# A four-layer graph network: keys first, shorter masks, joint finishing, output by two tiles, and products with the counts ahead of those with the mask

## The chip, the cores and the metric

The kernel runs on one NeuronCore of a Trainium2 chip. The metric is the time of one execution on the device, in microseconds (us); lower is better. Besides TensorE (matrix products; its weight loads are shown apart, as PEld) the core has VectorE (DVE), ScalarE (ACT), GpSimd (POOL) and SyncE (SP), which here issues most transfers.

## What is computed

A graph of 2500 nodes (256 features each) and 40000 edges passes through four blocks, each `x = x + layer(relu(layernorm(x)))`: two graph-attention layers with 8 heads of 32 features, a product with a 256 x 256 matrix built from the edges, three neighbour-mean layers with three dense layers, and a graph attention with 4 heads of 64. The core of an attention, per head:

```python
e = leaky_relu(el[src] + er[dst], 0.2)
ex = exp(e - segment_max(e, dst)[dst])
out = segment_sum((ex / segment_sum(ex, dst)[dst])[:, None] * h[src], dst)
x = elu(out + b)
```

The last attention has `exp(-leaky_relu(s))` with the roles of `src` and `dst` exchanged, and its result passes through `elu` twice (once per head, once over all heads) before the residual is added.

## The kernel before, in words

Nodes are padded to 20 tiles of 128 (`NT`, 2560 = `NP`). The kernel keeps a dense matrix of edge counts, `C[s, d]`, in f16 in on-chip memory: 20 source tiles by 2560 destinations.

*Start and building of C.* A first stage (lines 166 to 397) loads the edges, turns them and makes a table. The next (lines 439 to 612) goes through 40 windows of 64 destinations; for each, VectorE makes one-hot tiles (`ohc`, `ohl`), three in a ring, and TensorE multiplies them into `acc`; ScalarE copies the window to C. The same stage finds repeated edges: SyncE loads the keys of one round, `right` and `left` (L508, L510), TensorE compares them in `psD` (L604, L606) ahead of the window's own products (`three`, L589), and GpSimd scatters weights. `rows_in` (L159) loads x on the same SyncE queue.

*Attention* (`attention`, L630), called three times. After a layer norm (or the ELU of the layer before) and the product with the weights, factors are prepared: for an edge the weight is a product of a source factor (U or V) and a destination factor (F1 or F2), and which pair applies depends on the sign of `el + er`. So the sum over sources is a product with a *mask*: counts where the sum is positive, zero elsewhere, and one with the *counts* for the rest. The loop (from L997) goes over heads h, over `PARTS` of the destinations (2 halves of 1280 in attention 1 and 2, 4 quarters of 640 in attention 3, where `split` is set), and over the 20 source tiles s:

- ScalarE compares: `Rm` = relu(rows + bias), a huge number where the sum is positive (L1067);
- VectorE makes the mask `M` = min(Rm, C) (L1111). In attention 1 and 2 every fourth tile is made by VectorE alone, in one longer operation (L1114), except those in `MORE_ON_ACT`. In attention 3 twelve of twenty tiles also get `Mn` = C - M (L1101); the other eight, `TURNED`, use a product with C itself;
- TensorE multiplies the mask (L1198) and, for attention 1 and 2, the counts (L1206; in attention 3 for the tiles in `TURNED`, L1201) into eight banks, four for each of two parts in turn, with high and low halves of the factors side by side.

`Rm` and `M` have `SG` buffers (4; 5 in attention 3). ScalarE may start tile s when the mask of tile s - SG is made, VectorE when TensorE has finished with tile s - SG. TensorE waits in `cut` for the mask of its tile, and its semaphore `s_P` tells that the tile is done.

When a part is through, its sums are evacuated inside the next part, after `LEAD` tiles: ScalarE scales the low halves into `tl` (L1075), VectorE adds the high halves (L1138), multiplies by F2 and F1 (L1142, L1143), adds (L1147), and divides by the sum of the weights (L1152, L1156, L1160), one step after each mask. In attention 1 and 2 the result of the first half waits in `stash` and is copied after the second (L1165), since it overwrites factors that are still read. ScalarE issues its instructions in the order LEAD comparisons, evacuation, the others.

*End.* `elu` (L1217) applies the last activation in batches of four tiles, in two rounds with an exponential each; `write_result` loads x back in one transfer of 2.5 MB and writes the output in six, on GpSimd's queue.

Of the kernel before, what the change touches and what calls it, by code (L numbers as in the profile page):

```python
# [15 lines left out]
P = 128  # L16
N = 2500
E = 40000
D = 256
# [18 lines left out]
MORE_ON_ACT = {(0, 7), (1, 11)}  # L38
# [29 lines left out]
def build(nc, x, src, dst, ew, gat0, gat1, sage, dec, gat3, out):  # L68
# [4 lines left out]
    with top:  # L73
# [365 lines left out]
        with Phase() as ph:  # L439
# [52 lines left out]
            def _(sp):  # L492
                rows_in(sp, XB, x, s_x)
                for l, (Wx, gat) in enumerate(((Wx0, gat0), (Wx1, gat1))):
                    sp.dma_start(Wx[:, :, 0:D], gat[0].rearrange("(k p) f -> p k f", p=P)).then_inc(s_w, 16)
                    for j in range(2):
                        sp.dma_start(av[:, l, j, :], gat[1 + j].rearrange("(a h) d -> a (h d)", a=1)
                                     .to_broadcast([P, D])).then_inc(s_w, 16)
                sp.dma_start(bias[:, :], gat0[3].rearrange("(a f) -> a f", a=1).to_broadcast([P, D])).then_inc(s_w, 16)
# [130 lines left out]
        def attention(Wx, first, nh, dh, split, norm, sgn, scatter, next_bias=None):  # L630
# [181 lines left out]
            with heads as hp:  # L812
# [4 lines left out]
                F1, F2 = hp.sb("F1", [P, TH], f32), hp.sb("F2", [P, TH], f32)  # L817
# [5 lines left out]
                with Phase() as ph:  # L823
# [61 lines left out]
                    def _(v):  # L885
# [38 lines left out]
                        ch.wait()  # L924
                        v.tensor_scalar(kap[:, :], kap[:, :], TOP * LO, None, ALU.mult).then_inc(s_e, 1)
# [23 lines left out]
                    def _(a):  # L949
# [7 lines left out]
                        a.activation(F1[:, :], tt[:, :], ACT.Exp).then_inc(s_ex, 1)  # L957
                        a.activation(F2[:, :], tt2[:, :], ACT.Exp).then_inc(s_ex, 1)
# [38 lines left out]
                with Phase() as ph:  # L997
# [3 lines left out]
                    tl = ph.sb("tl", [P, RG, cw if split else 2 * cw], f32)  # L1001
                    stash = None if split else ph.sb("stash", [P, TP, dh], f32)
                    q1 = ph.sb("q1", [P, TP, cw], f32)
                    rec = ph.sb("rec", [P, TP], f32)
                    if scatter:
# [3 lines left out]
                    s_R, s_M, s_Mn, s_cut, s_P, s_E, s_tl, s_v, s_bias = (  # L1009
                        ph.sem(n) for n in ("R", "M", "Mn", "cut", "P", "E", "tl", "v", "bias"))  # L1010
# [51 lines left out]
                    def _(a):  # L1062
                        def steps(h, p, s0, s1):
                            for s in range(s0, s1):
                                if s in on_act[p]:
                                    cut(a, h * PARTS + p, s - SG, hold)
                                    a.activation(Rm[:, s % SG, :], rows[:, p % 2, :], ACT.Relu,  # L1067
                                                 bias=cB[:, ds(h + s * nh, 1)]).then_inc(s_R, 1)

                        def evacuate(h, p):  # L1070
                            q = h * PARTS + p
                            hold(a, s_P, (q + 1) * NT + SG)
                            hold(a, s_E, q + 2)
                            for r, n, part in banks(p % 2, 1):
                                ins = a.activation(tl[:, r:r + n, :], part, ACT.Copy, scale=1 / LO)  # L1075
# [13 lines left out]
                    def _(v):  # L1089
# [3 lines left out]
                        v.sem_inc(s_E, 2)  # L1093
                        ch = Chain(v, s_v)

                        def low_part(h, p, s):
# [3 lines left out]
                            Cs = C[:, s * NP + p * W:s * NP + (p + 1) * W]  # L1100
                            v.tensor_tensor(Mn[:, u, :], Cs, M[:, u, :], ALU.subtract).then_inc(s_Mn, 1)  # L1101

                        def steps(h, p, s0, s1, between=()):
                            between = list(between)
                            for s in range(s0, s1):
                                g, u = (h * PARTS + p) * NT + s, s % SG
                                Cs = C[:, s * NP + p * W:s * NP + (p + 1) * W]
                                if s in on_act[p]:
                                    v.wait_ge(s_R, compared(h, p, s) + 1)
                                    v.wait_ge(s_P, g + 1)  # L1110
                                    v.tensor_tensor(M[:, u, :], Rm[:, u, :], Cs, ALU.min).then_inc(s_M if s in ONE else s_cut, 1)  # L1111
                                else:
                                    v.wait_ge(s_P, g + 1)
                                    v.scalar_tensor_tensor(M[:, u, :], rows[:, p % 2, :], cN[:, ds(h + s * nh, 1)], Cs,  # L1114
# [9 lines left out]
                        def evacuation(h, p):  # L1124

                            q = h * PARTS + p
                            factor = lambda Fq: Fq[:, :].rearrange("p (t h) -> p t h", h=nh)[
# [52 lines left out]
                        for stage in stages + last:  # L1180
                            stage()
# [1077 lines left out]
```

## Time and profile before

| | |
|---|---|
| median of 3 runs | 2196.62 us (2195.84 to 2196.69) |
| the profiled execution | 2193.83 us, its span 2192.2 us, mean granted clock 0.940 |
| busy | TensorE 1747.3 (80%), VectorE 1618.4 (74%), ScalarE 1410.0 (64%), GpSimd 299.0 (14%) |
| stages | start to the first window 46.0; C 295.7; attention 1 prepared 79.9, loop 345.0; attention 2 prepared 76.4, loop 344.5; matrix, neighbour and dense layers with preparation of attention 3 690.5; loop of attention 3 271.8; end 42.4 |

A row of a timeline gives the start of an instruction, its duration, engine, line, what it writes and reads, and how long the engine stood idle before it. Durations of neighbours overlap by their latency; the distance from start to start is what an instruction takes of its engine. A row with xN is N such instructions in a row. The share of busy time is a mean over all stages; what counts is which engine fills a stage.

### The profile page before, as it was taken

The page shows a single profiled execution, that of the slowest core. Times are in us where ns is not written, and L with a number is a line of the kernel's source. Part 1 is how long each engine was busy: PE and PEld are TensorE (multiplying, and loading weights), DVE is VectorE, ACT ScalarE, POOL GpSimd, SP SyncE. Part 2 cuts the span into 40 slices and gives each one's busy share as a digit, 9 for nine tenths or more (in the row PEclk, how much of TensorE's full clock was granted, in tenths as well). Part 3 has the DMA queues.
Part 4 walks back from the last instruction along what each step waited for, and adds up shares of the span by engine and source line. Part 5 has one row for each costly group of instructions (what it writes and reads, how often), then busy time and mean ns, then how long its engine had stood idle before and what let it go on. Part 6 is the DMA issues. An engine that isn't in the chain of part 4 may idle for free. (4 is left out here: it accounts for less than half of the span.)

```text
span 2192.2 us, 64066 instructions
## 1 busy us (share of the span) xinstructions
PE 1747.3 (80%) x21987; PEld 1343.4 (61%) x21987; DVE 1618.4 (74%) x3673; ACT 1410.0 (64%) x2346; POOL 299.0 (14%) x457
## 2 busy tenths in 40 slices
PE   2998886298998855989885499998989984688881
PEld 1333334288888735888884356665548973688881
DVE  4988877899999978999999722222332257899997
ACT  0146675799999849999996712221213355899992
POOL 2465500466400011000000000000000001000000
PEclk9999998699999987999998799999999997899996
DMA  3000000010110000101011110000001010000102
GB/s 85 1 1 2 2 2 1 27 39 26 38 38 27 14 26 16 38 27 39 26 38 35 67 42 1 0 0 7 1 21 33 22 56 13 14 20 21 27 15 95
DMA packets 32298, 54.99 MB, mean 25 GB/s; under 512 B 10541, under 2 KB 23626, under 8 KB 31800
## 3 DMA queue, kind: packets, MB, share of 16 engines
q1 hardware_dynamic: 27848, 46.45, 6.5%
q0 software_dynamic: 4208, 5.24, 0.7%
q8 instruction: 160, 2.62, 0.5%
q14 instruction: 82, 0.67, 0.1%
HBM read 43.19 MB, written 8.49 MB: 24 GB/s over the span
## 5 line engine op out<-in xcount | busy, mean ns | idle before, releaser
L1198 PE MATMUL ps<-R,M 128*128 128x132 f16 (+1 forms) x8640 | 808.8, 221 | 202.7 <-DVE M L1111 101.9
L1067 ACT ACTIVATE Rm<-rows,cB 128x1280 bf16<-128x1280 f32 (+1 forms) x832 | 884.3, 1153 | 20.3 <-DVE Mn L1101 13.8
L1198 PEld LDWEIGHTS ps<-R,M 128*128 128x128 f16 x8640 | 728.8, 97 | 245.6 <-issue 115.2
L1206 PE MATMUL ps<-HB,C 128*128 128x66 f16 x6400 | 596.1, 193 | 0.0
L1111 DVE TENSOR_TENSOR M<-Rm,C 128x1280 f16<-128x1280 bf16 (+1 forms) x832 | 555.3, 691 | 41.0 <-ACT Rm L1067 37.4
L1206 PEld LDWEIGHTS ps<-HB,C 128*128 128x128 f16 x6400 | 571.7, 97 | 0.0
L1630 PE MATMUL psA<-R,C 128*128 128x512 f16 (+1 forms) x1200 | 253.0, 350 | 20.3 <-POOL ones L1664 9.5
L558 DVE TENSOR_SCALAR ohc<-cells,near 128x1280 f16<-128x1280 f16 x387 | 213.2, 551 | 58.4 <-PE acc L596 54.8
L596 PE MATMUL acc<-ohc,ohl 128*128 128x420 f16 (+1 forms) x1161 | 244.2, 348 | 1.6 <-DVE ohl L560 0.4
L1114 DVE SCALAR_TENSOR_TENSOR M<-rows,cN,C 128x1280 f16<-128x1280 f32 x128 | 197.9, 1546 | 0.0
L1630 PEld LDWEIGHTS psA<-R,C 128*128 (+1 forms) x1200 | 118.7, 99 | 117.5 <-issue 33.2
L596 PEld LDWEIGHTS acc<-ohc,ohl 128*128 128x128 f16 x1161 | 89.9, 98 | 148.6 <-DVE ohl L560 94.1
L423 POOL DMA_INDIRECT wd<-wv,wi x104 | 123.2, 1185 | 128.3 <-issue 71.6
L542 ACT ACTIVATE C<-acc 128x420 f16<-128x420 f32 (+1 forms) x120 | 55.7, 542 | 125.0 <-PE acc L596 125.0
L1781 DVE TENSOR_SCALAR rdeg<-psD 128x1 f32 (+1 forms) x20 | 3.2, 158 | 153.0 <-ACT tl L1746 153.0
L560 DVE TENSOR_SCALAR ohl<-lows,bT 128x128 f16<-128x128 f16 x387 | 101.5, 262 | 0.0
L1560 ACT ACTIVATE R<-L 128x256 f32 (+3 forms) x40 | 14.5, 363 | 129.8 <-DVE L L1792 80.3
L1101 DVE TENSOR_TENSOR Mn<-C,M 128x640 f16<-128x640 f16 x192 | 93.5, 487 | 0.6
L1201 PE MATMUL ps<-VS,C 128*128 128x130 f16 x640 | 88.7, 222 | 0.0
L1198 PE MATMUL ps<-R,Mn 128*128 128x130 f16 x960 | 86.8, 220 | 0.0
L1754 ACT ACTIVATE hT<-ps,b0c 128x128 f32<-128x128 f32 x80 | 22.9, 368 | 86.9 <-PE ps L1705 86.9
L1705 PE MATMUL ps<-xT,W 128*128 128x128 f32 x640 | 76.3, 278 | 1.6 <-ACT xT L1750 1.6
(300 smaller groups left out, 2333.9 us busy)
## 6 DMA issues: line engine op xcount, KB each, us to landing
rows<-rowd SPq DMA_DIRECT2D x32, 640.0 KB, 3.9
rows<-rowd SPq DMA_DIRECT2D x16, 320.0 KB, 3.5
xd<-R SPq DMA_DIRECT2D x4, 640.0 KB, 2.9
xr<-xd SPq DMA_DIRECT2D x20, 128.0 KB, 2.0
xd<-HB SPq DMA_DIRECT2D x1, 2560.0 KB
xr<-xd POOLq DMA_DIRECT2D x1, 2560.0 KB, 9.2
R<-in_x SPq DMA_DIRECT2D x1, 2432.0 KB
xr<-in_x SPq DMA_DIRECT2D x19, 128.0 KB, 2.0
```

Of the source, the lines that this page charges most:

```text
L423: g.indirect_dma_start(out=wd[:, :], out_offset=bass.IndirectOffsetOnAxis(ap=m["wi"][w][:, :], axis=0), in_=m["wv"][w][:, :], in_offset=No ...
L558: v.tensor_scalar(ohc[:, u, :], cells[:, :], near[:, q % 2, ds(k, 1)], None, ALU.is_equal).then_inc(s_oh, 1)
L560: v.tensor_scalar(ohl[:, u, :], lows[:, :], bT[:, ds(k, 1)], None, ALU.is_equal).then_inc(s_oh, 1)
L596: ins = pe.matmul(bank(b, q % 2), ohl[:, u, :], ohc[:, u, d0 * NT:d1 * NT], start=first_, stop=True, skip_group_check=True)
L1067: a.activation(Rm[:, s % SG, :], rows[:, p % 2, :], ACT.Relu, bias=cB[:, ds(h + s * nh, 1)]).then_inc(s_R, 1)
L1101: v.tensor_tensor(Mn[:, u, :], Cs, M[:, u, :], ALU.subtract).then_inc(s_Mn, 1)
L1111: v.tensor_tensor(M[:, u, :], Rm[:, u, :], Cs, ALU.min).then_inc(s_M if s in ONE else s_cut, 1)
L1114: v.scalar_tensor_tensor(M[:, u, :], rows[:, p % 2, :], cN[:, ds(h + s * nh, 1)], Cs, ALU.is_gt, ALU.mult).then_inc(s_M, 1)
L1198: m = pe.matmul(region(p % 2, r), lhsT, rhs, start=first, stop=True, skip_group_check=True)
L1201: m = pe.matmul(region(p % 2, r), C[:, s * NP + p * W + (r % TP) * P:][:, 0:P], VS[:, TURNED.index(s), :, ds(h * cw, cw)], start=False, st ...
L1206: m = pe.matmul(both[:, :, cw:2 * cw], C[:, s * NP + p * W + r * P:][:, 0:P], VP[:, s, :, ds(h * cw, cw)], start=False, stop=True, skip_gr ...
L1630: m = pe.matmul(psA[:, :], lhsT, SPv[:, s, :, :].rearrange("p l c -> p (l c)"), start=s == 0, stop=s == NT - 1)
```

## The change

Five parts:

1. *Keys first*: SyncE issues the keys of the first two windows before x and the weights (`later_loads`).
2. *Shorter masks*: in the last part of each head, comparison and masks cover only the destinations that exist, `wide(p)`: 1220 in place of 1280, 580 in place of 640. The factors of the padding are made zero by two more small operations before the exponentials. TensorE still multiplies whole tiles; `MORE_ON_ACT` loses tile 11 of the second half, so VectorE makes that mask alone.
3. *Joint finishing*: `tl` holds two parts; the additions are still made for each part, the other steps once for two (the factors are one tensor, F12). `stash` and the copy from it are gone.
4. *Output by two tiles*: the last stage is a pipeline over ten pairs of tiles, with three activations on ScalarE and two operations on VectorE for each; x comes back in five transfers and the output leaves in eleven, all on SyncE's queue.
5. *Counts ahead of the mask*: TensorE makes a source tile's products with the counts first, and waits for the mask only then. In attention 3 the regions are also numbered by tile and side in turn.

```diff
-MORE_ON_ACT = {(0, 7), (1, 11)}
+MORE_ON_ACT = {(0, 7)}
...
-                rows_in(sp, XB, x, s_x)
-                for l, (Wx, gat) in enumerate(((Wx0, gat0), (Wx1, gat1))):
...
+                def later_loads():
+                    rows_in(sp, XB, x, s_x)
+                    for l, (Wx, gat) in enumerate(((Wx0, gat0), (Wx1, gat1))):
...
+                    if q == 1:
+                        later_loads()
...
+                        for q in (tt, tt2):
+                            ch(v.tensor_scalar(q[:, TH - nh:TH], q[:, TH - nh:TH], padneg[:, 0:1], None, ALU.add))
+                        ch.wait()
...
+                    wide = lambda p: W - (NP - N if p == PARTS - 1 else 0)
...
-                                    a.activation(Rm[:, s % SG, :], rows[:, p % 2, :], ACT.Relu,
+                                    a.activation(Rm[:, s % SG, 0:wide(p)], rows[:, p % 2, 0:wide(p)], ACT.Relu,
...
-                            hold(a, s_E, q + 2)
+                            hold(a, s_fin, h * (PARTS // 2) + p // 2 + 1)
...
-                                ch(v.tensor_tensor(xv, xv, factor(F2), ALU.mult))
-                                ch(v.tensor_tensor(q1[:, :, :], xu, factor(F1), ALU.mult))
+                                ch(v.tensor_tensor(both(tl), both(tl), factors, ALU.mult))
...
+                                ch(v.tensor_tensor(both(tl)[:, :, 0], both(tl)[:, :, 0], both(tl)[:, :, 1], ALU.add))
...
-                                ch(v.tensor_copy(room[:, 0:TP, ds(h * cw, dh)], stash[:, :, :]))
...
+                            return [add] + ([scale, total, weight, inverse, mean] if p % 2 else [])
...
+                                    for r in range(RG):
+                                        side, d = sides(r)
+                                        if split and side and s in TURNED:
+                                            pe.matmul(region(p % 2, r), Cd(d), VS[:, TURNED.index(s), :, ds(h * cw, cw)],
+                                                      start=False, stop=True, skip_group_check=True)
+                                        if not split:
+                                            both = region(p % 2, r).rearrange("p (l c) -> p l c", l=2)
+                                            pe.matmul(both[:, :, cw:2 * cw], Cd(d), VP[:, s, :, ds(h * cw, cw)],
+                                                      start=opens and r % 3 == 0, stop=True, skip_group_check=True)
                                     cut(pe, q, s, lambda eng, sem, value: eng.wait_ge(sem, value))
                                     for r in range(RG):
...
+                def negative(k):
+                    if k >= 4:
+                        a.wait_ge(s_u, k - 3)
+                    a.activation(e(k), of_heads(k), ACT.Relu, scale=-1.0).then_inc(s_r, 1)
+
+                def power(k):
+                    a.wait_ge(s_r, k + 1)
+                    a.activation(e(k), e(k), ACT.Exp, scale=-1.0).then_inc(s_e, 1)
+
+                def again(k):
+                    a.wait_ge(s_e, k + 1)
+                    a.activation(e(k), e(k), ACT.Exp, bias=minus[:, 0:1]).then_inc(s_ee, 1)
...
+                def unit(k):
+                    v.wait_ge(s_ee, k + 1)
+                    v.scalar_tensor_tensor(y(k).rearrange("p (h c) -> p h c", c=64), e(k), -1.0, of_heads(k), ALU.add,
+                                           ALU.max).then_inc(s_u, 1)
+
+                def residual(k):
+                    v.wait_ge(s_u, k + 1)
+                    if 2 * k % TB == 0:
+                        v.wait_ge(s_xr[2 * k // TB], 16)
+                    v.tensor_tensor(y(k), y(k), xr[:, 2 * k * D:(2 * k + 2) * D], ALU.add).then_inc(s_y, 1)
```

How the instructions stand. First SyncE at the beginning of the stage that builds C, before (`right` and `left` are the keys, `flat` their source, `R` takes x):

```order
L491 UNCONDITIONAL_BRANCH
L161 DMA R<-in_x 128x19x256
L163 DMA R<-in_x 68x256
L495 DMA Wx<-in_L_gnn_W 128x2x256
L497 DMA HB<-in_L_gnn_al 128x256
...
L499 DMA bias<-in_L_gnn_b 128x256
L462 TENSOR_LOAD table
...
L508 DMA right<-flat 2x512
L510 DMA left<-flat 4x128
```

and with the change:

```order
L491 UNCONDITIONAL_BRANCH
L462 TENSOR_LOAD table
...
L510 DMA right<-flat 2x512
L512 DMA left<-flat 4x128
...
L506 COMPARE_AND_BRANCH
L161 DMA R<-in_x 128x19x256
L163 DMA R<-in_x 68x256
L496 DMA Wx<-in_L_gnn_W 128x2x256
```

Two windows' keys now stand in front of the nine other loads. Next TensorE at the first source tile of attention 1, before (`HB` holds the factors that go with the counts `C`, `R` those that go with the mask `M`; ps00 to ps03 are the banks):

```order
L1198 MATMUL ps00_145<-R,M_131 128x132
L1206 MATMUL ps00_145<-HB,C 128x2x33
...
L1198 MATMUL ps01_146<-R,M_131 128x132
L1206 MATMUL ps01_146<-HB,C 128x2x33
...
L1198 MATMUL ps03_148<-R,M_131 128x132
L1206 MATMUL ps03_148<-HB,C 128x2x33
```

and with the change:

```order
L1205 MATMUL ps00_142<-HB,C 128x2x33 x3
L1205 MATMUL ps01_143<-HB,C 128x2x33 x3
L1205 MATMUL ps02_144<-HB,C 128x2x33 x3
L1205 MATMUL ps03_145<-HB,C 128x2x33
L1212 MATMUL ps00_142<-R,M_130 128x132 x3
L1212 MATMUL ps01_143<-R,M_130 128x132 x3
L1212 MATMUL ps02_144<-R,M_130 128x132 x3
L1212 MATMUL ps03_145<-R,M_130 128x132
```

Ten products with the counts, then ten with the mask, where one followed the other in turn. Last VectorE in the body of attention 1's loop over heads, in the first half, after five masks; before:

```order
L1138 TENSOR_TENSOR tl<-ps_152,tl 128x66
...
L1142 TENSOR_TENSOR tl<-tl,F_96 128x10x33
...
L1143 TENSOR_TENSOR q_134<-tl,F_95 128x330
...
L1147 TENSOR_TENSOR q_134<-q_134,tl 128x330
...
L1160 TENSOR_TENSOR R<-q_134,rec 128x10x32
...
L1165 COPY R<-stash 128x10x32
```

and with the change:

```order
L1146 TENSOR_TENSOR tl<-ps_149,tl 128x66
...
L1154 TENSOR_TENSOR tl<-tl,F_95 128x1320
...
L1158 TENSOR_TENSOR tl<-tl 128x20x33
...
L1170 TENSOR_TENSOR R<-tl,rec 128x20x32
```

Between the rows shown stand the masks of the running half, one after each step. The steps are fewer and twice to four times as long, and after the second half's additions (the other place) only masks follow.

## Rows read from the trace of the kernel before

**Rows 1.** Busy time by stage: stretch, length, busy us of each engine, granted clock, DMA.
```profile
421.60:766.60 345.00, 305.37 (x6400) 289.10 (x6400) 334.07 (x488) 335.80 (x320) 102.44 (x120) 0.98 0.09 29
...
1878.00:2149.80 271.80, 234.99 (x3840) 224.24 (x3840) 253.71 (x672) 248.04 (x384) 0.00 (x0) 0.98 0.07 20
2149.80:2192.20 42.40, 0.00 (x0) 0.00 (x0) 30.74 (x61) 10.46 (x10) 5.21 (x7) 0.50 0.31 122
```

**Rows 2.** Timeline of SyncE at the start: start, duration, what is issued.
```profile
30.85 0.40 SPq L161 DMA_DIRECT2D R<-in_x  x1
...
37.62 0.43 SPq L499 DMA_DIRECT2D bias<-in_L_gnn_b  x1
39.71 0.32 SPq L508 DMA_DIRECT2D right<-flat  x1
```

**Rows 3.** Timeline of TensorE at the start, idle time before it behind.
```profile
45.98 0.59 PE L604 MATMUL psD<-notlater,big 128*128 128x512 f16 x1 [26.32 <-DMA left<-flat]
```

**Rows 4.** DMA issues of the page: count, KB each, us from issue to landing.
```profile
xr<-xd SPq DMA_DIRECT2D x20, 128.0 KB, 2.0
...
xr<-xd POOLq DMA_DIRECT2D x1, 2560.0 KB, 9.2
```

**Rows 5.** Timeline of ScalarE, attention 1.
```profile
445.44 0.88 ACT L1075 ACTIVATE tl<-ps 128x198 f32<-128x198 f32 x4
...
467.48 20.16 ACT L1067 ACTIVATE Rm<-rows,cB 128x1280 bf16<-128x1280 f32 x16
487.66 0.91 ACT L1075 ACTIVATE tl<-ps 128x198 f32<-128x198 f32 x4
```

**Rows 6.** Timeline of VectorE, attention 1.
```profile
603.91 1.54 DVE L1114 SCALAR_TENSOR_TENSOR M<-rows,cN,C 128x1280 f16<-128x1280 f32 x1
605.37 2.29 DVE L1111 TENSOR_TENSOR M<-Rm,C 128x1280 f16<-128x1280 bf16 x3
...
617.15 1.03 DVE L1138 TENSOR_TENSOR tl<-ps,tl 128x198 f32<-128x198 f32 x4
618.10 0.81 DVE L1111 TENSOR_TENSOR M<-Rm,C 128x1280 f16<-128x1280 bf16 x1
618.83 0.49 DVE L1142 TENSOR_TENSOR tl<-tl,F 128x330 f32<-128x330 f32 x1
```

**Rows 7.** Timeline of TensorE, attention 1.
```profile
599.84 0.22 PE L1198 MATMUL ps<-R,M 128*128 128x132 f16 x1
599.89 0.19 PE L1206 MATMUL ps<-HB,C 128*128 128x66 f16 x1
599.92 0.22 PE L1198 MATMUL ps<-R,M 128*128 128x132 f16 x1
```

**Rows 8.** Timeline of TensorE's weight loads, attention 1.
```profile
599.89 0.10 PEld L1198 LDWEIGHTS ps<-R,M 128*128 128x128 f16 x1
```

**Rows 9.** Timeline of ScalarE, attention 3.
```profile
1946.03 0.85 ACT L1075 ACTIVATE tl<-ps 128x195 f32<-128x195 f32 x4
1946.78 5.14 ACT L1067 ACTIVATE Rm<-rows,cB 128x640 bf16<-128x640 f32 x7
1952.58 9.86 ACT L1067 ACTIVATE Rm<-rows,cB 128x640 bf16<-128x640 f32 x13 [0.66 <-DVE Mn L1101]
```

**Rows 10.** Timeline of VectorE, attention 3.
```profile
1945.30 0.89 DVE L1111 TENSOR_TENSOR M<-Rm,C 128x640 f16<-128x640 bf16 x2
```

**Rows 11.** Timeline of ScalarE, before attention 2.
```profile
770.34 0.42 ACT L744 ACTIVATE e<-z 128x256 f32<-128x256 f32 x1 [0.22 <-DVE z L684]
770.66 0.40 ACT L748 ACTIVATE e<-e 128x256 f32<-128x256 f32 x1
```

**Rows 12.** Timeline of ScalarE, last stage.
```profile
2152.36 2.00 ACT L1308 ACTIVATE e<-e 128x1024 f32<-128x1024 f32 x2 [6.25 <-DVE e L1262]
```

**Rows 13.** Timeline of VectorE, last stage.
```profile
2151.43 1.74 DVE L1262 TENSOR_SCALAR e<-HB 128x256 f32<-128x256 f32 x8 [1.60 <-PEq L101]
...
2184.86 1.23 DVE L1291 SCALAR_TENSOR_TENSOR R<-e,R 128x1024 f32<-128x1024 f32 x1
```

More of the change, by code:

```diff
@@ L1130, in evacuation @@
                             room = HB[:, 0:NT * nh * cw] if split else R[:, :]
                             room = room.rearrange("p (t c) -> p t c", t=NT)
-                            held = not split and p == 0
-                            o = stash[:, :, :] if held else room[:, p * TP:(p + 1) * TP, ds(h * cw, dh)]
                             def add():
                                 hold(v, s_tl, q + 1)
-                                for r, n, part in banks(p % 2, 0):
-                                    ch(v.tensor_tensor(tl[:, r:r + n, :], part, tl[:, r:r + n, :], ALU.add))
+                                parts = list(banks(p % 2, 0))
@@ L1149, in weight @@
                             def weight():
-                                hold(v, s_E, q + 3)
-                                ch(v.tensor_scalar(rec[:, :], q1[:, :, dh], 1e-30, None, ALU.max))
+                                ch.wait()
+                                ch(v.tensor_scalar(rec[:, :], both(tl)[:, :, 0, dh], 1e-30, None, ALU.max))
                             def inverse():
@@ L1159, in mean @@
                                 ch.wait()
-                                ch(v.tensor_tensor(o, q1[:, :, 0:dh], rec[:, :].unsqueeze(2).to_broadcast([P, TP, dh]),
-                                                   ALU.mult))
-                            def unstash():
-                                ch.wait()
-                                ch(v.tensor_copy(room[:, 0:TP, ds(h * cw, dh)], stash[:, :, :]))
-                            stages = [add, scale, both, weight, inverse, mean]
-                            return stages, [unstash] if not split and p == 1 else []
+                                v.tensor_tensor(room[:, some, ds(h * cw, dh)], both(tl)[:, :, 0, 0:dh],
+                                                rec[:, :].unsqueeze(2).to_broadcast([P, 2 * TP, dh]), ALU.mult).then_inc(s_fin, 1)
+                            return [add] + ([scale, total, weight, inverse, mean] if p % 2 else [])
                         def rest(h, p, before):
-                            stages, last = evacuation(*before) if before else ([], [])
-                            steps(h, p, LEAD, NT, stages + last)
+                            steps(h, p, LEAD, NT, evacuation(*before) if before else [])
                         body = parts_in_order(v, steps, rest)
                         with v.Fori(1, nh) as h:
-                            ch.begin(h - 1, PARTS * (NB + 5) + (0 if split else 1))
+                            ch.begin(h - 1, PARTS * (NB - 1) + PARTS // 2 * 4)
                             body(h, False)
                             ch.end(nh - 1)
-                        stages, last = evacuation(nh - 1, PARTS - 1)
-                        for stage in stages + last:
+                        for stage in evacuation(nh - 1, PARTS - 1):
                             stage()
@@ L1192, in _ @@
                                     cut(pe, q, s, lambda eng, sem, value: eng.wait_ge(sem, value))
                                     for r in range(RG):
-                                        first = s == 0 and r % 3 == 0
-                                        side = r // TP if split else 0
-                                        lhsT = (Mn if side and s in TWO else M)[:, s % SG, (r % TP) * P:(r % TP + 1) * P]
+                                        side, d = sides(r)
+                                        lhsT = (Mn if side and s in TWO else M)[:, s % SG, d * P:(d + 1) * P]
```

204 lines of the change are left out of this document (75 added, 129 removed).

## The prediction

> **What bounds the kernel now.** I read four views, in this order: the busy time of each engine by stage, the timelines of each engine inside a stage, the order of the instructions, and the waits. The stages first [rows 1]. In the first attention loop ScalarE is busy 335.80 of 345.00 us and VectorE 334.07, TensorE 305.37 at granted clock 0.98: two engines tie for the bound and TensorE has a tenth to spare. The second attention runs the same loop. In the third (1878.0 to 2149.8) VectorE and ScalarE are again ahead of TensorE, 253.71 and 248.04 of 271.8 us, and neither fills them. In the last stage (42.4 us) TensorE does nothing and VectorE works 30.74 us. The chain of waits of the page covers only that last stage, so it says nothing about the loops.
>
> At the start, SyncE issues the loads of x and of weights from 30.85 and comes to the first keys only at 39.71 [rows 2]; TensorE starts at 45.98, after 26.32 us of idleness that ended with the keys' landing [rows 3]. Nothing else is late there.
>
> **Keys first.** SyncE was free at 30.85 [rows 2]. It still has to read its table (the last earlier issue, 37.62, ended at 38.05 and the keys came at 39.71: 1.7 us), then issues three small transfers at about 0.35 us each, and they need to land. For the landing the bounds are 0 and the 5 us that it took behind 2.4 MB of x; the nearest row is a 128 KB piece with 2.0 us [rows 4], and I take 2.0. So 30.85 + 1.7 + 1.0 + 2.0 = 35.5 in place of 45.98: **-10.5 us**. The x load and weights now go behind the second keys; nobody needs them before the stage ends, and the next keys are asked for only after the first window's matrix products. They cost nothing; without that cover the cost would be the same 10 us again. What is late next is TensorE and VectorE themselves, which share this stage.
>
> **The loops of attention 1 and 2.** One head is two halves of ten destination tiles. Before, ScalarE's evacuations begin at 445.44 and, two halves later, at 487.66 [rows 5]: 42.2 us a head. ScalarE's own sum: 16 comparisons in 20.18 us (467.48 to 487.66), 1.26 each, plus the evacuation, 0.91 of which 0.14 overlap the next comparison: 0.77. So 2 x 20.95 = 41.9. VectorE's [rows 6]: a mask from ScalarE's comparison takes (2.29 - 0.81)/2 = 0.74, one made by VectorE alone 605.37 - 603.91 = 1.46, so 16 x 0.74 + 4 x 1.46 = 17.7 a half; the evacuation 0.95 for the additions (617.15 to 618.10, so the four overlap what follows by 0.08), 0.49 - 0.08 = 0.41 for each of four operations on 330 elements (320 for the last), about 0.25 for two small ones, and once a head a copy out of the stash, below 0.3. That is 35.4 + 5.7 and the copy, some 41.3. ScalarE sets the pace, VectorE is half a microsecond behind.
>
> After. First half: ScalarE 20.2 + 0.77 = 20.95. VectorE 17.68 + 0.95 + the joint finishing of the head before: 330 elements take 0.41, of which 330 at 0.96 per ns are 0.34 and 0.07 is fixed (an estimate from these rows, since one element a cycle is what 0.41 allows), so 1320 elements take 1.44, 660 take 0.76, 640 take 0.74, and two small ones 0.25: 3.19. Sum **21.8**, VectorE's. Second half, 1220 columns in place of 1280: ScalarE has 15 comparisons (one was given back to VectorE) at 1.26 - 0.05 = 1.21, and the evacuation, 18.95. VectorE 15 x 0.71 + 5 x 1.40 + 0.95 = 18.6. Sum **18.95**, ScalarE's. In the first half ScalarE may run ahead by its four buffers, so a wait there costs it nothing later. A head takes 40.75 in place of 42.22, 1.47 less; 16 heads in the two layers **-23.5**. At the end of each layer the joint finishing stands bare, about 0.9 more: **+1.8**. Bounds: if every wait were filled, VectorE's sum 40.4 would hold, -1.8 a head, -29; a head now takes 0.3 more than the longer sum, and if it loses twice that on top of mine, it gains 0.9, -14.
>
> **Counts ahead of the mask.** TensorE makes for each source tile ten products with the mask and ten with the counts, now in turn. A pair takes 0.08 to 0.09 us (599.84 to 599.92) [rows 7], twenty 0.9 us, against 40.75/40 = 1.02 us per tile that VectorE needs on the mean. No row of VectorE in the loops waits for TensorE. So the regrouping shortens only what comes after a mask (0.57 in place of 0.9): nothing in the steady state, 0.3 us at the end of each layer, **-0.6**. This holds if ten short products in a row keep the 0.03 us that each has now. The trace has no such row. The nearest: the load for the mask product starts at 599.89 [rows 8], together with the count product before it, and the mask product starts at 599.92 [rows 7]. A load is thus followed by its product after 0.03 us, although its row says 0.10, and the load of a count product would do likewise. Bounds: 0.03 and the 0.057 of a wide product. I take 0.033, and the sum is unchanged.
>
> A rule speaks against this. The Trainium skill ("TensorE: Matmul & The Clock Gate", section on fast weight load) puts an ordinary load of 128 columns at 128/1.2 = 107 ns and the fast form at a measured factor of about 2, which makes some 53 ns a load, an estimate from that page. The rows contradict it, since two loads here fit into 90 ns; by the page the change would come out as the second rival.
>
> **Attention 3.** Four quarters of five tiles a head. ScalarE: (5.14 - 0.82)/6 = 0.72 (0.82 being one with its overlap) a comparison, 20 of them and 0.75 for the evacuation: 15.15 [rows 9]. VectorE: 32 operations at 0.40 [rows 10] and 2.8 for the evacuation: 15.6. A quarter takes 16.3 (1946.03 to the end of the thirteen comparisons at 1962.3 [rows 9]): both lose, because during the evacuation ScalarE comes to the end of its five buffers (0.66 of waiting before 1952.58) and VectorE then waits for it. The joint finishing makes the burst after a pair 4.05 in place of 2.8 and leaves 0.95 in the other quarter. Walked through tile by tile, ScalarE's tile 14 waits for the second mask of tile 9, and tile 17 for that of tile 12: 2.4 us in one quarter and none in the other, 15.15 x 2 + 2.4 = 32.7 against 32.5. Eight pairs: +1.6. The last quarter is 580 columns: 20 x 0.05 less for ScalarE, -1.0 a head, -4.0. The end stands bare with +1.3. Together **-1**. Bounds -6 and +8.
>
> **Before the loops**: two small operations and a wait in front of the exponentials, about 0.25 in each of three attentions, **+0.8**.
>
> **The last stage.** Before, 42.4 us from 2149.8 [rows 1], of which 1.6 are VectorE's wait at the change of stage [rows 13]. Now three activations on 512 elements for each of ten pairs. A Relu on 256 takes 0.32 (770.34 to 770.66) [rows 11], an exponential on 1024 takes 2.00 - 1.06 = 0.94 [rows 12]; between them 512 takes 0.53. The third has its bias in memory, like the comparisons of 1280 and 640 elements (1.26 and 0.72: 0.54 for 640 elements, so 0.18 fixed against 0.11 in the others), 0.6 to 0.65. Sum 1.7 a pair, **17.1**. VectorE needs 2 x 0.6, less, so ScalarE sets the pace. Start 0.3, the last pair's two operations 1.5, stores and end 4.5 (a store of 128 KB 2.0 [rows 4] and two issues; bound above 6.1, from VectorE's last operation, over at 2186.1 [rows 13], to the end at 2192.2). 23.4 against 40.8: **-17.4**.
>
> **Sum.** -10.5 - 23.5 + 1.8 - 0.6 - 1 + 0.8 - 17.4 = -50.4. The profiled execution took 2193.83, so 2143.4; the median of the runs is 2.8 above it, 2196.62, which gives **2146 us**.
>
> **Rivals.** *The bursts eat the loops' gain*: four buffers do not let ScalarE run ahead, and what VectorE saves comes back as waits as in attention 3. For: there it is so already. Against: in attention 1 and 2 ScalarE would have to wait 1.5 us a head more than its slack of 0.85 in the first half. The loops give nothing: 2146 + 24 = 2170. *Loads of weights bind TensorE* (the other side): for, there is no row of short products in a row. With the 0.057 of a wide product a tile takes 1.14, a head 45.6, 3.4 more than now, 16 heads +54; with the rest of the change, 2196.6 - 26.9 + 54 = 2224. It decides from about 0.053 us a product on (1.10 a tile, 44 a head, +1.8 x 16 = +28); that is the page's estimate, and the time would be 2198. *The last stage is bound by transfers*: x comes back in pieces through the queue that carries the stores, 9.2 us in all now [rows 4]; if stores wait behind it the stage gains 10, and 2153 results. *The loops reach VectorE's sum*: 2140, inside the forecast's bounds. *The change doesn't do what it says*: the order shows keys, counts and finishing moved, so this is left with almost nothing.
>
> **How the numbers follow.** The forecast with its bounds 0.73, the transfers 0.08, the bursts 0.11, TensorE slower than now 0.04, TensorE at the page's value 0.03, the rest 0.01. A measurement of this kernel tells 0.2% (4.4 us) from no change. Faster 0.93, same 0.03, slower 0.04. The range: below, the loops at -29 and attention 3 at -5, 2136, and a little for keys and end, 2134; above it reaches to the bursts, 2170.
>
> **What would show it.** Right: TensorE's first product at 35 to 36 us; comparisons of 1220 columns; a head of 40.5 to 41 us; count products 0.03 apart; three ScalarE activations per pair and about 23 us after the last barrier. Wrong: count products 0.05 or more apart, VectorE waiting for TensorE in the loops, a head above 42, or a last stage above 30.

## The result and the profile after

The changed kernel takes **2142.6 us** (median of 4 runs, 2141.3 to 2144.0) beside 2196.2 for the kernel before: a ratio of 0.976 (0.974 to 0.978), 54 us less. 2146 was forecast. The profiled execution spans 2142.2 us against 2192.2, so the traces account for 50.0 us; the execution profiled before lay 2.4 us below its median, the one after 1.4 above. Cut at the same events in both, from the start of each stage to the start of the next:

| stretch | before | after | difference | forecast |
|---|---|---|---|---|
| start to TensorE's first `psD` | 45.98 | 34.72 | -11.3 | -10.5 |
| to the first comparison of attention 1 | 375.63 | 376.91 | +1.3 | } +0.8 in all |
| between the loops of attention 1 and 2 | 76.54 | 77.45 | +0.9 | } |
| loops of attention 1 and 2 | 345.01, 344.37 | 332.12, 332.12 | -25.1 | -22.3 |
| neighbour and dense layers, attention 3 prepared | 690.62 | 694.63 | +4.0 | } |
| loop of attention 3 | 271.67 | 269.12 | -2.6 | -1.0 |
| end | 42.38 | 25.13 | -17.3 | -17.4 |

The sum is right within half a microsecond (-50.0 against -50.4), but that is partly luck: the loops, the start and attention 3 gave 5 us more than forecast, and stretches that I had costed at 0.8 became 6.2 longer. Of these 6.2, up to 3.8 may come from which execution of each kernel was profiled. In medians the change gave 53.6 us, 3 more than the sum.

The busy time by stage of the kernel after, to be laid beside [rows 1] (stretch, length, busy us of TensorE, its weight loads, VectorE, ScalarE, GpSimd; granted clock, DMA):

```profile
411.63:743.75 332.12, 299.37 (x6400) 290.45 (x6400) 325.02 (x424) 319.01 (x312) 118.39 (x120) 0.98 0.09 30
...
1847.95:2117.07 269.12, 232.17 (x3840) 225.59 (x3840) 247.88 (x616) 241.45 (x384) 0.00 (x0) 0.98 0.06 20
2117.07:2142.20 25.13, 0.00 (x0) 0.00 (x0) 12.77 (x21) 16.62 (x30) 0.10 (x1) 0.50 0.57 206
```

In the first loop VectorE issues 424 instructions in place of 488 and leads ScalarE by 6 us, where both were level before. In the last stage ScalarE (16.62) has taken over from VectorE (30.74 before).

The start, SyncE's and then TensorE's timeline, answering to [rows 2] and [rows 3]:

```profile
32.38 0.33 SPq L510 DMA_DIRECT2D right<-flat  x1
32.81 0.71 SPq L512 DMA_DIRECT2D left<-flat  x2
...
37.29 0.43 SPq L161 DMA_DIRECT2D R<-in_x  x1
```

```profile
34.72 0.59 PE L608 MATMUL psD<-notlater,big 128*128 128x512 f16 x1 [15.14 <-DMA left<-flat]
```

The keys are issued at 32.38, near the 32.55 worked out (30.85 and 1.7), and TensorE starts 1.2 after the last of them was issued, where I had allowed 2.0. It still waits for them, 15.14 us in place of 26.32.

ScalarE in attention 1, answering to [rows 5]:

```profile
556.89 0.91 ACT L1083 ACTIVATE tl<-ps 128x198 f32<-128x198 f32 x4
557.66 18.31 ACT L1075 ACTIVATE Rm<-rows,cB 128x1220 bf16<-128x1220 f32 x15
575.86 0.88 ACT L1083 ACTIVATE tl<-ps 128x198 f32<-128x198 f32 x4
576.61 12.75 ACT L1075 ACTIVATE Rm<-rows,cB 128x1280 bf16<-128x1280 f32 x10
590.02 7.48 ACT L1075 ACTIVATE Rm<-rows,cB 128x1280 bf16<-128x1280 f32 x6 [0.66 <-DVE M L1120]
597.43 0.91 ACT L1083 ACTIVATE tl<-ps 128x198 f32<-128x198 f32 x4
```

A head takes 40.54 us (556.89 to 597.43; 42.22 before). A row names the shape of its first instruction: three of the fifteen comparisons from 557.66 on already belong to the next, wider half. One half is ScalarE's, 18.97 from evacuation to evacuation (556.89 to 575.86). In the other it stops once for 0.66 us, at the end of its four buffers, when VectorE has gone through its burst. That burst, answering to [rows 6]:

```profile
580.71 1.53 DVE L1154 TENSOR_TENSOR tl<-tl,F 128x1320 f32<-128x1320 f32 x1
582.15 0.82 DVE L1120 TENSOR_TENSOR M<-Rm,C 128x1280 f16<-128x1280 bf16 x1
582.89 0.84 DVE L1158 TENSOR_TENSOR tl<-tl 128x660 f32<-128x660 f32 x1
583.64 0.82 DVE L1120 TENSOR_TENSOR M<-Rm,C 128x1280 f16<-128x1280 bf16 x1
```

From start to start the joint steps take 1.44 and 0.75; 1.44 and 0.76 were worked out from the rows for 330 elements.

TensorE on one source tile, answering to [rows 7], and its weight loads, answering to [rows 8]:

```profile
575.17 0.47 PE L1205 MATMUL ps<-HB,C 128*128 128x66 f16 x10
575.47 0.74 PE L1212 MATMUL ps<-R,M 128*128 128x132 f16 x10
576.05 0.47 PE L1205 MATMUL ps<-HB,C 128*128 128x66 f16 x10
```

```profile
575.11 0.40 PEld L1205 LDWEIGHTS ps<-HB,C 128*128 128x128 f16 x10
```

Ten products with the counts, each with a load of its own, start within 0.30 us (575.17 to 575.47), ten with the mask within 0.58: a tile takes 0.88, as it did in turn.

Attention 3, ScalarE, answering to [rows 9]:

```profile
2088.24 2.43 ACT L1075 ACTIVATE Rm<-rows,cB 128x640 bf16<-128x640 f32 x3 [1.54 <-DVE Mn L1110]
2091.13 6.96 ACT L1075 ACTIVATE Rm<-rows,cB 128x640 bf16<-128x640 f32 x10 [0.46 <-DVE Mn L1110]
2097.99 0.85 ACT L1083 ACTIVATE tl<-ps 128x195 f32<-128x195 f32 x4
```

The two stalls behind the joint burst are there, 2.0 us together in this quarter. Over the whole loop ScalarE waits 18.7 us for VectorE's `Mn`, 2.3 for each of the eight bursts; before the change it waited 13.8.

The last stage, ScalarE's and VectorE's timelines in its middle and near its end, and the page's row of the transfers, answering to [rows 4], [rows 12] and [rows 13]:

```profile
2122.15 0.61 ACT L2165 ACTIVATE R<-HB 128x512 f32<-128x512 f32 x1
2122.67 0.61 ACT L2169 ACTIVATE R<-R 128x512 f32<-128x512 f32 x1
2123.19 0.70 ACT L2173 ACTIVATE R<-R,minus 128x512 f32<-128x512 f32 x1
2123.80 0.61 ACT L2165 ACTIVATE R<-HB 128x512 f32<-128x512 f32 x1
```

```profile
2133.84 0.69 DVE L2186 SCALAR_TENSOR_TENSOR R<-R,HB 128x512 f32<-128x512 f32 x1 [0.36 <-ACT R L2173]
```

```profile
xr<-xd SPq DMA_DIRECT2D x5, 512.0 KB, 5.4
```

A pair of tiles takes ScalarE 1.65 us (2122.15 to 2123.80), and VectorE waits for it. The pieces of x need 5.4 us to land but no row of VectorE in this stage waits for a transfer.

### The profile page after: what moved, and what is told of

Same layout as the page of the kernel before. It is cut to its first block and busy times, and to the rows that moved or that the text cites. A ratio compares the mean times of both kernels' runs of the same rounds, so it can differ in the third digit from the quotient of the medians.

```text
span 2142.2 us, 63551 instructions
## 1 busy us (share of the span) xinstructions
PE 1738.8 (81%) x21987; PEld 1353.1 (63%) x21987; DVE 1579.4 (74%) x3455; ACT 1375.7 (64%) x2350; POOL 309.4 (14%) x451
## 5 line engine op out<-in xcount | busy, mean ns | idle before, releaser
L1075 ACT ACTIVATE Rm<-rows,cB 128x1280 bf16<-128x1280 f32 (+3 forms) x816 | 847.0, 1132 | 32.0 <-DVE Mn L1110 18.7
L1212 PE MATMUL ps<-R,M 128*128 128x132 f16 (+1 forms) x8640 | 684.5, 221 | 120.1 <-DVE Mn L1110 66.1
L1212 PEld LDWEIGHTS ps<-R,M 128*128 128x128 f16 x8640 | 545.6, 97 | 144.1 <-DVE M L1120 51.0
L1120 DVE TENSOR_TENSOR M<-Rm,C 128x1280 f16<-128x1280 bf16 (+3 forms) x816 | 529.3, 678 | 36.7 <-ACT Rm L1075 30.1
L1205 PE MATMUL ps<-HB,C 128*128 128x66 f16 x6400 | 304.9, 195 | 66.7 <-DVEq L1101 66.7
L1205 PEld LDWEIGHTS ps<-HB,C 128*128 128x128 f16 x6400 | 259.5, 98 | 66.9 <-DVEq L1101 66.9
L1542 PE MATMUL psA<-R,C 128*128 128x512 f16 (+1 forms) x1200 | 253.5, 350 | 21.6 <-POOL ones L1576 9.5
L1123 DVE SCALAR_TENSOR_TENSOR M<-rows,cN,C 128x1280 f16<-128x1280 f32 (+1 forms) x144 | 217.9, 1513 | 0.0
L1212 PE MATMUL ps<-R,Mn 128*128 128x130 f16 x960 | 126.5, 221 | 0.0
L1212 PEld LDWEIGHTS ps<-R,Mn 128*128 128x128 f16 x960 | 93.1, 97 | 0.0
L1110 DVE TENSOR_TENSOR Mn<-C,M 128x640 f16<-128x640 f16 (+1 forms) x192 | 92.0, 479 | 0.6
```

The lines of the kernel that those rows point to most:

```text
L1075: a.activation(Rm[:, s % SG, 0:wide(p)], rows[:, p % 2, 0:wide(p)], ACT.Relu, bias=cB[:, ds(h + s * nh, 1)]).then_inc(s_R, 1)
L1110: v.tensor_tensor(Mn[:, u, 0:wide(p)], Cs, M[:, u, 0:wide(p)], ALU.subtract).then_inc(s_Mn, 1)
L1120: v.tensor_tensor(M[:, u, 0:wide(p)], Rm[:, u, 0:wide(p)], Cs, ALU.min).then_inc(s_M if s in ONE else s_cut, 1)
L1123: v.scalar_tensor_tensor(M[:, u, 0:wide(p)], rows[:, p % 2, 0:wide(p)], cN[:, ds(h + s * nh, 1)], Cs, ALU.is_gt, ALU.mult).then_inc(s_M, 1)
L1205: pe.matmul(both[:, :, cw:2 * cw], Cd(d), VP[:, s, :, ds(h * cw, cw)], start=opens and r % 3 == 0, stop=True, skip_group_check=True)
L1212: m = pe.matmul(region(p % 2, r), lhsT, rhs, start=split and opens and r % 3 == 0, stop=True, skip_group_check=True)
```

## Experiments

The loop lengths below are from the first comparison of the attention to the last instruction of its finishing. Medians compare with 2142.6. The runs were made on three chips, on which the kernel before had medians of 2195.9 to 2197.1, so differences of about 1 us between medians say nothing; the loop lengths, which repeat within 0.3, are the better measure. Joint finishing in attention 1 and 2 and the new numbering of the regions in attention 3 were not undone by themselves.

**One part at a time.** *The keys behind x and the weights again:*

```diff
+                later_loads()
                 sp.sem_inc(s_D, 1)
...
-                    if q == 1:
-                        later_loads()
```

> The changed kernel with x and the weights ahead of the keys again, the rest as changed. My theory: TensorE's first product starts near 46 us in place of 34.7 and attention 1's first comparison comes 10 to 11 us later than 411.6, so the time is 10 us above the changed kernel's (about 2153). Rival: another wait in the stage that builds C takes up most of the head start; then the first comparison moves by less than 5 us.

Measured 2155.8 (ratio to before 0.981, 0.980 to 0.983), 13.2 more, where 10 was expected; the profiled executions differ by 10.2. In the trace TensorE starts at 46.74 in place of 34.72:

```profile
46.74 0.58 PE L607 MATMUL psD<-notlater,big 128*128 128x512 f16 x1 [27.15 <-DMA left<-flat]
```

The first comparison of attention 1 comes 10.9 us later than in the changed kernel (the stretch up to it took 375.8 in place of 376.9, and between 375.2 and 377.0 in all runs), and the loops and the end keep their lengths within 0.3. So no other wait takes the place of this one: it is on the path, nearly all of it.

*Only the new end, in the kernel before* (the pipeline over ten pairs in place of `elu` and `write_result`):

```diff
-        with Phase() as last:
...
+        with Phase() as ph:
+            PAIRS, TB = NT // 2, 4
...
```

> The kernel before with the new last stage alone. My theory: the last stage takes 25 us in place of 42.4, and the time is 17 us below the kernel before (about 2179). Rival: its gain hangs on the rest (the finishing of attention 3, or the state in which the transfers' queue is found), and alone it gives 10 us or less.

Measured 2179.4 (0.993, 0.991 to 0.994), 17.7 less than the kernel before beside it; the end takes 24.91 us, 25.13 in the changed kernel. So these two parts keep their worth without the rest.

*Masks of full width again:*

```diff
-                    wide = lambda p: W - (NP - N if p == PARTS - 1 else 0)
+                    wide = lambda p: W
```

> The changed kernel with comparisons and masks of full width in the last part of each head. My theory: in attention 1 and 2 the second half is ScalarE's, 15 x 0.05 us longer, so a head takes 0.75 more and 16 heads 12 us; in attention 3 the last quarter is 1.0 longer, 4 us; together 16 us above the changed kernel. Rival: VectorE is the bound throughout; the two engines save nearly the same there, so the total could be told apart only by ScalarE still waiting for VectorE in the second half; if another wait hides the width, below 5 us.

Measured 2157.7 (0.982, 0.980 to 0.983), 15.1 more, 16 expected. Loops 338.02 and 337.91 (+5.9, +5.8), attention 3 273.23 (+4.1).

*Tile 11 of the second half compared by ScalarE again:*

```diff
-MORE_ON_ACT = {(0, 7)}
+MORE_ON_ACT = {(0, 7), (1, 11)}
```

> The changed kernel with the comparison of tile 11 of the second half on ScalarE again. My theory: ScalarE sets the second half, so it takes 1.2 us more, 19 us in 16 heads. Rival: VectorE bounds both halves (its sum 40.4 is the measured head of 40.5); then giving it 0.7 us less to do makes a head shorter, by up to 0.5 us, 8 us in all.

Measured 2163.4 (0.985, 0.983 to 0.986), 20.8 more (19 expected), loops 341.74 and 341.70. The second half now lies open as ScalarE's; VectorE's timeline there:

```profile
571.60 0.80 DVE L1120 TENSOR_TENSOR M<-Rm,C 128x1220 f16<-128x1220 bf16 x1 [0.41 <-ACT Rm L1075]
```

One comparison more, 1.20 us a head, costs 9.6 a loop in eight heads: all of it. So the small edit of one tile is worth more than the shorter masks: without it VectorE, whose work in this half the joint finishing has cut, waits for ScalarE there.

The prices of the parts do not add up to the gain. From evacuation to evacuation the second half went from 21.27 to 18.97 us and the first from 20.95 to 21.57, since the whole finishing now stands there (in the kernel before, the evacuation between 445.44 and 487.66 [rows 5] is this one):

```profile
466.71 0.91 ACT L1075 ACTIVATE tl<-ps 128x198 f32<-128x198 f32 x4 [0.23 <-issue]
```

Over 16 heads that is 36.8 gained and 9.9 given back. Undoing the widths and the tile (11.7 and 19.2 in both loops) acts on the second half alone, and so shows nothing of what was given back.

**The order of TensorE's products.** *Counts in turn with the mask again:*

```diff
-                                    for r in range(RG):
-                                        side, d = sides(r)
...
-                                            pe.matmul(both[:, :, cw:2 * cw], Cd(d), VP[:, s, :, ds(h * cw, cw)],
...
-                                        m = pe.matmul(region(p % 2, r), lhsT, rhs, start=split and opens and r % 3 == 0, stop=True,
+                                        m = pe.matmul(region(p % 2, r), lhsT, rhs, start=opens and r % 3 == 0, stop=True,
...
+                                            m = pe.matmul(both[:, :, cw:2 * cw], Cd(d), VP[:, s, :, ds(h * cw, cw)],
```

> The changed kernel with the products of mask and counts in turn again, both behind the wait for the mask. My theory: the loops are bound by VectorE and ScalarE, a head stays at 40.5 us and the time within 1.5 us of the changed kernel's. Rival: doing the counts while the mask is made is what shortens the loops (VectorE gets its buffer back earlier); then a head takes 41.2 us or more and the time is 10 us or more above.

Measured 2147.6 (0.977, 0.976 to 0.979), 5.0 more; loops 334.72 and 334.71, 2.6 more each. Neither number was right. ScalarE's timeline shows what I had missed:

```profile
591.07 7.48 ACT L1075 ACTIVATE Rm<-rows,cB 128x1280 bf16<-128x1280 f32 x6 [0.66 <-DVE M L1120]
598.79 0.91 ACT L1083 ACTIVATE tl<-ps 128x198 f32<-128x198 f32 x4 [0.24 <-PE ps L1210]
```

Once a head the evacuation comes up before TensorE has finished the half. With the counts first, only 0.58 us of products follow the last mask in place of 0.88, and this wait is gone. A head takes 40.84 in place of 40.54, of which the wait is 0.24 to 0.26. To test this, two kernels in which the evacuation comes one tile later, with either order:

```diff
-                LEAD = 7 if split else 4
+                LEAD = 7 if split else 5
```

With the counts in turn:

> Counts in turn with the mask, and in attention 1 and 2 the evacuation of a part begins after five tiles of the next part, not four. Theory (in e2 ScalarE's evacuation stood 0.24 to 0.3 us a head waiting for TensorE's last products): that wait goes, both loops come back to 332.1 to 332.6 (334.7 in e2), and the time falls by 4 to 5 against e2, to about 2143. Rival (the 0.3 us a head is lost elsewhere, for instance where VectorE's masks wait for TensorE to free a buffer): the loops stay at 334 to 335, time 2147 to 2148.

With the counts ahead:

> The changed kernel with the evacuation after five tiles in attention 1 and 2: the control for the run before. Theory: ScalarE's evacuations do not wait there for TensorE, so nothing is to be gained; loops 332.1 within 0.5, time 2142 to 2143. If instead the fifth tile itself helps, the loops would fall here as much as they do between e2 and the run before, 2.3 each, to 330.

Measured 2150.5 and 2148.1 (0.979 and 0.979, each within 0.002), loops 335.3 and 335.0 (the rest of their distance lies outside the loops). Both numbers missed: 2142 to 2143, with loops of about 332.1 to 332.6, was expected of either. The later place has a price of its own: ScalarE's waits for VectorE over the loop go from 4.6 to 6.8 us (the view of waits from 415 to 740 us, with the sum, the number and the longest, of the changed kernel and then of the second of these two; in the first they are 6.8 and 3.9):

```profile
ACT Rm L1075 <- DVE M L1120: 4.6, 7, 0.7
ACT tl L1083 <- PE ps L1212: 3.4, 1, 3.4
```

```profile
ACT Rm L1075 <- DVE M L1120: 6.8, 14, 0.7
ACT tl L1083 <- PE ps L1212: 3.6, 1, 3.6
```

But the difference between the two orders speaks to the question. With the evacuation after four tiles it is 2.6 us a loop, and with the counts in turn (the run before these two) ScalarE waits for TensorE seven times in that window:

```profile
ACT tl L1083 <- PE ps L1210: 1.7, 7, 0.3
```

After five tiles ScalarE never waits for TensorE but at the very end, and the difference between the orders is 0.3 us a loop, that of the bare end alone (3.9 against 3.6). So the order of the products is worth mainly what it takes from the evacuation's wait: 1.7 and 0.3 of the 2.6 us show as such waits, and the other 0.6 is not located. It is not shown that nothing else is gained: after five tiles ScalarE's longer waits for VectorE could hide a smaller effect.

**Attention 3.** *One finishing step after every second tile:*

```diff
-                                if between:
+                                if between and (not split or s % 2):
```

> The changed kernel, but in attention 3 a step of the finishing stands only after every second mask (tiles 7, 9, 11, 13, 15, 17) in place of after each from tile 7. My theory: the burst of VectorE work is what makes ScalarE run out of its five buffers, 2.4 us a pair; spread out, VectorE's lag stays within them and the loop of attention 3 gets 5 to 10 us shorter than 269.1 us. Rival: the quarters are bound by the sums of the two engines, and ScalarE's waits only shift; then the loop stays within 2 us.

Measured 2139.8 (0.974, 0.973 to 0.975); loop 266.07, 3.05 less than 269.12. That is less than the 5 to 10 expected and more than the rival's 2.

*Finishing of each quarter by itself* (the multiplication by both factors stays one operation, unlike before the change; only the last line of the edit is shown):

```diff
...
-                            return [add] + ([scale, total, weight, inverse, mean] if p % 2 else [])
+                            return [add] + ([scale, total, weight, inverse, mean] if p % 2 or split else [])
...
```

> The changed kernel with the finishing of attention 3 done for each quarter apart (attention 1 and 2 still jointly, three in place of five operations of a part merged as in the change). My theory: the joint finishing costs there, 1.6 us in the pairs and 1.3 at the end, so the loop takes about 3 us less than 269.1. Rival: VectorE's busy time counts, and with four more small operations a pair the loop takes 3 to 5 us more.

Measured 2140.5 (0.975, 0.974 to 0.976); loop 267.45, 1.7 less, where 3 was expected. *Both:*

```diff
...
-                                if between:
+                                if between and (not split or s % 2):
...
-                            return [add] + ([scale, total, weight, inverse, mean] if p % 2 else [])
+                            return [add] + ([scale, total, weight, inverse, mean] if p % 2 or split else [])
```

> Both edits of attention 3 together: the finishing is made for each quarter by itself and one step after every second tile. Theory (what attention 3 loses is ScalarE at the end of its buffers during a burst): e5 gave 3.05 and e6 1.7 of the loop's 269.12; together the waits of both quarters nearly go and the loop comes to 263.5 to 265.5, time 2136 to 2138. Rival (the two edits remove the same wait): the loop stays at 266, and the separate steps cost 0.5 a head on VectorE, so 266 to 268, time 2139 to 2141.

Measured **2136.1** (2134.7 to 2139.7; 0.973, 0.972 to 0.975), loop 263.87. The gains add up (3.05 and 1.7, together 5.25), so the two edits remove different losses. The waits of ScalarE over the loop, in the changed kernel and in this one:

```profile
ACT Rm L1075 <- DVE Mn L1110: 18.7, 19, 1.8
```

```profile
ACT Rm L1075 <- DVE Mn L1110: 8.2, 12, 2.2
```

The waits fell by twice what the loop gained; where the other half went is not shown. This kernel is the fastest on record, by 7.7 us against the changed kernel in runs on the same chip (next run), of which the loop is 5.1; the rest lies in stages that the edit does not touch. In attention 3 the joint finishing was a loss that the shorter quarter covered up: with full masks the changed loop takes 273.23, more than the 271.67 before the change.

**The changed kernel once more.**

> The changed kernel once more, not altered, to see how far a stage moves from one profile to the next. If the stretch between attention 2 and the loop of attention 3 (694.63 in the changed kernel, 690.62 before, code the same) varies from run to run, it shows another length here, by 1 to 4 us; if it belongs to the kernel, it shows 694.6 within 0.3. Loops 332.1, time 2142 to 2143 in both cases.

Measured 2143.8 (2143.3 to 2144.2), loops 332.24 and 332.12, the stretch between attention 2 and 3 694.25. That is within 0.4 of 694.63, which would mean that the +4.0 there belongs to the kernel. Other runs contradict it. The kernel with only the new end has the same instructions as the kernel before up to that end, and its stretch took 692.43 in place of 690.62. The changed kernel and the three runs that alter only the loop of attention 3 show 694.6, 694.3, 693.6 and 693.3. So this stage moves by up to 2 us between profiles of the same code.

## Why the prediction was right

- **Keys first**, -10.5: -11.3. The landing after the last issue took 1.2, where 2.0 was taken, between the bounds of 0 and 5. TensorE's first product, at 34.72, came just before the 35 to 36 given as a sign.
- **Head of 40.75**: 40.54. The second half, ScalarE's 18.95, measured 18.97. The first was put at 21.8 as VectorE's sum and measured 21.57, of which an estimate puts 0.15 down to four masks between two evacuations that already belong to the narrower half (3 at 0.03 less and one at 0.06 less). 16 heads at 0.21 are 3.4 us, of which the loops show 2.8 beyond the forecast. The edges of a loop came out as forecast, 0.6 longer: 332.12 - 8 x 40.54 = 7.8 against 345.01 - 8 x 42.22 = 7.25.
- **Widths and tile 11**: 5.9 and 9.6 a loop when undone. The sum per half, of the longer engine, predicts both within 0.2.
- **Counts ahead of the mask**, -0.6: the right sum for the wrong setting. I looked for a wait of VectorE for TensorE, found none, and concluded that the regrouping does nothing in the steady state. The step failed: it ignored ScalarE's evacuation, which has to wait for the last product. In the kernel before it did not wait (its waits from 415 to 740 us show none for TensorE); with the gain of the other parts it would have. The order is worth 2.6 a loop in the changed kernel. My sum did not suffer, because a head of 40.75 already assumed that nothing waits.
- **Loads of weights bind TensorE**: falls. A count product with its load takes 0.030, for which 0.033 was taken. The estimate of some 53 ns a load, worked out in the prediction from the Trainium skill ("TensorE: Matmul & The Clock Gate", section on fast weight load), is refuted here. The same page of the Trainium skill ("TensorE: Matmul & The Clock Gate", section "Back-to-back issue gap") gives about 81 ns for a sustained pair of load and product of 128 columns; the pairs of 132 columns here take 58.
- **Attention 3**, -1: -2.6, inside its bounds. Stalls of 2.4 a pair were forecast and are 2.3 on the mean (18.7 in eight). What I did not draw from this is that the stalls were mine to spend: they are larger than what the joint steps save.
- **The end**, 25.0: 25.13. ScalarE's activations were put at 1.7 a pair and take 1.65. The Trainium skill ("ScalarE: Activation LUTs", "What ACT_TABLE_LOAD costs") has 186 ns and 0.833 an element with an immediate bias, 93 ns more for one in memory, and an overlap of 93 between neighbours. The trace agrees: 0.61 and 0.70 for 512 elements, 0.52 and 0.61 from start to start (2122.15 to 2123.80 above).
- **The stretches outside the loops**: +0.8 forecast, +6.2 measured, the largest miss. The step at fault is that I took unchanged code to keep its time. The two small operations and their wait take 0.40 in each attention (1813.28 to 1813.68):

```profile
1813.28 0.36 DVE L930 TENSOR_SCALAR tt<-tt,padneg 128x4 f32<-128x4 f32 x2
1813.68 0.15 DVE L932 TENSOR_SCALAR kap<-kap 128x1 f32<-128x1 f32 x1
```

That is 1.2 in three attentions. Of the other 5.0, 3.6 lie between attention 2 and 3. Lay ScalarE's 634 instructions of this stretch side by side in both traces: their distances agree but at a few places, and at most of these the granted clock differs. Two of them, each from the same instruction to the same instruction, in the kernel before, in the changed kernel, and in its second profile (columns as in the table of stages above; the last but two is the granted clock):

```profile
1205.04:1227.26 22.22, 5.73 (x23) 4.45 (x24) 14.37 (x53) 11.10 (x27) 0.00 (x0) 0.55 0.18 50
1764.99:1786.62 21.63, 16.05 (x184) 14.83 (x183) 9.41 (x24) 9.71 (x28) 4.45 (x1) 1.00 0.31 128
```

```profile
1171.01:1194.88 23.87, 7.25 (x23) 5.53 (x24) 14.37 (x53) 11.09 (x28) 0.00 (x0) 0.52 0.15 47
1732.52:1755.63 23.11, 17.54 (x183) 16.34 (x182) 9.39 (x24) 9.99 (x28) 4.45 (x1) 0.93 0.29 120
```

```profile
1170.66:1194.57 23.91, 7.24 (x23) 5.57 (x24) 14.37 (x53) 11.10 (x27) 0.00 (x0) 0.52 0.17 47
1732.94:1754.56 21.62, 16.04 (x184) 14.83 (x183) 9.41 (x24) 9.70 (x27) 4.45 (x1) 1.00 0.31 127
```

TensorE's busy time for the same products grows by as much as the place gets longer: 5.73 to 7.25 for 22.22 to 23.87, and 16.05 to 17.54 for 21.63 to 23.11, with more of the time at 1.2 GHz in place of 2.4. In all thirteen traces the second place takes 21.6 us at a clock of 1.00 or 23.1 to 23.5 at 0.93, whatever the kernel. And the two profiles of the changed kernel differ in it, 23.11 and 21.62; another place, 39.73 and 40.46, makes up for half of that. Their agreement within 0.4 was in part a coincidence. So a large part of what this stretch varies by, from 690.6 to 696.0 us in the thirteen traces, goes with where TensorE's clock is low. What decides that, and what is left of the +4.0 for the change itself, stays open.

## What to carry to other kernels

Where two engines alternate in setting the pace, make the sum for each part by itself and move work until each part's longer sum is shortest: one tile moved between engines was worth 19 us in the changed kernel, and costs one number. After that, ask of every wait, not only of the busiest engine's, how much slack it has left once the others are faster: TensorE's order caused no wait before and cost 5 us after. And where an engine runs ahead by a few buffers, several operations joined into one save their fixed parts, but the longer burst can use up those buffers: in attention 3, apart and spread out was faster by 5 us of loop. Last, before a difference in unchanged code is explained, look at it in a second profile of the same code, place by place.

## What the runs showed of the hardware that was not expected

Ten weight loads of 128 columns with products of 66 columns pass in 0.30 us (0.030 each), though a load's row says 0.10 and a product's 0.19. And the same code, with the same data, took 690.6 to 696.0 us for one stretch: its length changes by 1 to 2 us at a few places, among them those where the granted clock is lower in one execution than in another (at 0.93 in place of 1.00, one place took 23.11 us in place of 21.62).
